# Adapter and expert products: the first product into one accumulator of 256 columns

## What is computed

```
y = einsum('bsi,boi->bso', x, weight[itok])      # x 8 x 256 x 1024, weight 8 x 1024 x 1024
base = einsum('bth,oh->bto', y, W_up)
top1 = argmax(y @ gate_w.T + expert_bias)
delta = ((y @ lora_A[e].T) @ lora_B[e].T for e = top1) # 4 experts, rank 8
out = x + base + delta
```

## Time and profile before

| | |
|---|---|
| three runs | 397.61, 398.24, 399.97 us |
| profiled execution, span from first to last instruction | 397.9 us |
| PE matmuls busy | 379.4 us (95%), 2240 instructions |
| PE weight loads busy | 355.0 us (89%), 2240 instructions |
| VectorE (DVE) busy | 213.9 us (54%) |
| ScalarE (ACT) busy | 145.4 us (37%) |
| GpSimd (POOL) busy | 17.5 us (4%) |

### The profile page before, as it was taken

How to read it: one execution, slowest core, us unless ns; L and a number is a source line. 1 busy time by engine, 2 the same in 40 slices (tenths; PEclk the granted TensorE clock), 3 DMA queues, 4 the chain that set the end, 5 groups by cost and what they waited for, 6 DMA issues and landing times.

```text
span 397.9 us, 6753 instructions
## 1 busy us (share of the span) xinstructions
PE 379.4 (95%) x2240; PEld 355.0 (89%) x2240; DVE 213.9 (54%) x484; ACT 145.4 (37%) x316; POOL 17.5 (4%) x17
## 2 busy tenths in 40 slices
PE   2899869999999999999999999999999999999996
PEld 2689759889998999889998899988999899988996
DVE  3768495645546347456366455473573553654132
ACT  4766620637015340356105470153503452053100
POOL 0007520000000000000000000000000000000000
PEclk9999988999999999999999999999999999999999
DMA  6897856652096322971257611864229712450002
GB/s 187 300 360 224 261 216 190 239 203 82 24 285 202 146 105 84 273 230 45 105 137 283 213 50 55 248 225 160 105 60 267 234 71 105 146 170 0 0 0 105
DMA packets 21365, 63.65 MB, mean 160 GB/s; under 512 B 2544, under 2 KB 3696, under 8 KB 21360
## 3 DMA queue, kind: packets, MB, share of 16 engines
q1 hardware_dynamic: 21072, 63.07, 47.8%
q10 hardware_dynamic: 288, 0.52, 0.4%
HBM read 55.20 MB, written 8.39 MB: 160 GB/s over the span
## 4 chain that ended last, share of the span: by engine, by line
PE 87%; DMA 4%; DVE 4%; ACT 2%; SPq 1%; issue 1%; POOL 1%; ACTq 0%
PE ps_o L461 31%; PE ps_y L450 28%; PE ps_y L452 14%; PE ps_o L470 13%; PE ps_o L485 2%; DMA w_raw<-w_dram 2%; DMA lb_raw<-lora_b_dram 2%; DVE w_lo L346 2%; DVE x_hilo L339 1%; ACT up_hi L280 1%; POOL up_lo L244 1%; PE ps_y L478 0%; SPq L133 0%; SPq L149 0%; SPq L197 0%
## 5 line engine op out<-in xcount | busy, mean ns | idle before, releaser
L450 PE MATMUL ps_y<-x_hilo,w_hi 128*128 128x512 f32 x512 | 180.3, 397 | 9.4 <-DVE w_lo L346 7.8
L452 PE MATMUL ps_y<-x_hilo,w_lo 128*128 128x256 f32 x512 | 142.7, 279 | 0.0
L450 PEld LDWEIGHTS ps_y<-x_hilo,w_hi 128*128 128x128 f32 x512 | 96.8, 189 | 32.7 <-issue 7.4
L452 PEld LDWEIGHTS ps_y<-x_hilo,w_lo 128*128 128x128 f32 x512 | 97.0, 189 | 0.0
L346 DVE TENSOR_TENSOR w_lo<-w_raw,w_hi 128x512 fp32r<-128x512 f32 x128 | 81.4, 686 | 3.5 <-ACT w_hi L276 1.3
L461 PE MATMUL ps_o<-up_hi,y_hi 128*128 128x366 f32 x256 | 75.9, 337 | 1.9 <-POOL up_lo L244 1.9
L461 PE MATMUL ps_o<-up_lo,y_hi 128*128 128x366 f32 x256 | 74.8, 333 | 0.0
L461 PE MATMUL ps_o<-up_hi,y_lo 128*128 128x366 f32 x256 | 74.8, 333 | 0.0
L276 ACT CAST w_hi<-w_raw 128x512 fp32r<-128x512 f32 x128 | 71.3, 621 | 2.3 <-DMA w_raw<-w_dram 2.1
L296 ACT COPY y_small<-ps_y 128x256 f32<-128x256 f32 x64 | 23.8, 372 | 121.4 <-PE ps_y L452 121.4
L396 DVE TENSOR_TENSOR y_full<-ps_y,y_small 128x256 f32<-128x256 f32 x64 | 27.1, 424 | 68.8 <-ACT y_small L296 68.8
(11 more groups left out here) (33 smaller groups left out, 177.8 us busy)
## 6 DMA issues: line engine op xcount, KB each, us to landing
w_raw<-w_dram SPq DMA_DIRECT2D x63, 512.0 KB, 4.1
rows<-x_dram SPq DMA_DIRECT2D x16, 512.0 KB, 5.3
x_raw<-xT_dram SPq DMA_DIRECT2D x30, 256.0 KB, 7.0
up_raw<-w_up_dram SPq DMA_DIRECT2D x8, 512.0 KB, 6.7
out_dram<-rows SPq DMA_DIRECT2D x8, 512.0 KB, 7.7
out_dram<-rows SPq DMA_DIRECT2D x8, 329.0 KB, 7.2
out_dram<-rows SPq DMA_DIRECT2D x8, 183.0 KB, 6.7
x_raw<-xT_dram ACTq DMA_DIRECT2D x2, 256.0 KB, 3.4
```

The lines of the kernel that those rows point to most:

```text
L450: pe.matmul(ps_y[c % 2][:, :], w_hi[:, c % RING, cols], x_hilo[:, k, :], start=(k == 0), stop=False)
L452: last = pe.matmul(ps_y[c % 2][:, S:2 * S], w_lo[:, c % RING, cols], x_hilo[:, k, 0:S], start=False, stop=(k == KC - 1))
```

## The change

The first product adds its three terms into one accumulator, 256 columns of the bank. A step is three matmuls of 256 columns, with w_hi, w_hi and w_lo as weights. `y_small` and `y_full` go, with their semaphores. ScalarE casts `y_hi` out of PSUM; VectorE takes `y_lo` as PSUM minus `y_hi`, and PE may write the bank again after `y_ready`.

```diff
 # ScalarE, per chunk
                     act.wait_ge(y_done, b * OC + c + 1)
-                    act.copy(y_small[:, c % 2, :], ps_y[c % 2][:, S:2 * S]).then_inc(y_small_ready, 1)
+                    act.copy(y_hi[:, c, :], ps_y[c % 2][:, 0:S]).then_inc(y_hi_ready, 1)
                     if c < OC - RING:
                         w_hi_part(b, RING + c)
-                    act.wait_ge(y_full_ready, b * OC + c + 1)
-                    act.copy(y_hi[:, c, :], y_full[:, c % 2, :]).then_inc(y_hi_ready, 1)
 # VectorE, per chunk
-                    dve.wait_ge(y_small_ready, b * OC + c + 1)
-                    if c >= 2 or not first:
-                        dve.wait_ge(y_hi_ready, b * OC + c - 1)
-                    dve.tensor_tensor(y_full[:, c % 2, :], ps_y[c % 2][:, 0:S], y_small[:, c % 2, :],
-                                      ALU.add).then_inc(y_full_ready, 1)
+                    dve.wait_ge(y_hi_ready, b * OC + c + 1)
+                    dve.tensor_tensor(y_lo[:, c, :], ps_y[c % 2][:, 0:S], y_hi[:, c, :].bitcast(F32),
+                                      ALU.subtract).then_inc(y_ready, 1)
                     if c < OC - RING:
                         w_lo_part(b, RING + c)
-                    dve.wait_ge(y_hi_ready, b * OC + c + 1)
-                    dve.tensor_tensor(y_lo[:, c, :], y_full[:, c % 2, :], y_hi[:, c, :].bitcast(F32),
-                                      ALU.subtract).then_inc(y_ready, 1)
 # TensorE, first_product
                     if c >= 2:
-                        pe.wait_ge(y_full_ready, b * OC + c - 1)
+                        pe.wait_ge(y_ready, b * OC + c - 1)
...
-                        pe.matmul(ps_y[c % 2][:, :], w_hi[:, c % RING, cols], x_hilo[:, k, :],
+                        pe.matmul(ps_y[c % 2][:, 0:S], w_hi[:, c % RING, cols], x_hilo[:, k, 0:S],
                                   start=(k == 0), stop=False)
-                        last = pe.matmul(ps_y[c % 2][:, S:2 * S], w_lo[:, c % RING, cols], x_hilo[:, k, 0:S],
+                        pe.matmul(ps_y[c % 2][:, 0:S], w_hi[:, c % RING, cols], x_hilo[:, k, S:2 * S],
+                                  start=False, stop=False)
+                        last = pe.matmul(ps_y[c % 2][:, 0:S], w_lo[:, c % RING, cols], x_hilo[:, k, 0:S],
                                          start=False, stop=(k == KC - 1))
```

More of the change, by code:

```diff
@@ L66, in build @@
         gl_raw = sb("gl_raw", [P, OC, GL])
-        y_small = sb("y_small", [P, 2, S])
-        y_full = sb("y_full", [P, 2, S])
         y_hi = sb("y_hi", [P, OC, S], F32R)
@@ L112, in build @@
         y_done = sem("y_done")
-        y_small_ready = sem("y_small_ready")
-        y_full_ready = sem("y_full_ready")
         y_hi_ready = sem("y_hi_ready")
```

## The result

The changed kernel takes 402.64 us (median of four runs, 401.99 to 404.35) against 398.73 us for the kernel before, whose median has a fourth run since: a ratio of 1.0105, with a 95% interval of 1.0076 to 1.0135. It is slower, by about 4 us, where 1.5 us less was forecast. That lies inside the range that the forecast gave, but on the side of its rival 1.

A forecast was written before the change was run, and what follows sets the result against it. PE bounds the kernel: batches 1 to 7 are matmuls end to end, 46.71 us a batch. 397.9 (span) - 1.2 (batch 0) - 0.2 (PE's stream) + 0.3 (span to median) = 396.8, said as 396.7; range 393.2 to 403.5.

The forecast's parts named there:

- rival 1: First product: weight load, not column count, sets the pace; 0.122 us a matmul, +8.6 us, 405.4; chance 0.22 in some strength.
- PE's stream: First product, batches 1 to 7: time goes by columns, three 256s at 0.1155 us, 0.3465 a step, -0.2 us in all.
- The bounds: First product, a 256 behind a 256: between 0.113 and 0.122 us, taken as 0.1155.
- Starts 0.12 us and more apart: Sign in the profile after: such starts in a row of 256s would prove the weight load sets the pace.
- rival 2: First product: pace falls to the load's own 0.113 us, -8 ns a step, -3.6 us, 393.4; chance 0.10.
- Batch 0: Without the join, ScalarE's up_hi casts and the up_lo chain come earlier: -1.2 us, bounds 0.8 to 1.9.
- The first half of the route: Batch 0: y_hi without the join lets up_hi casts start earlier; GpSimd's up_lo(3) ends at 34.9 instead of 36.08, 1.2 us.
- The second half of the route: Batch 0 behind up_lo(3): DMAs and all after move by 1.2 us; up_lo wait some 0.7, z_parts wait still 3.7.
- The covered join: Batches 1 to 7: the join's copy and add lie under a full PE, so removing them gains nothing.
- the bank's new wait: PE's wait for y_ready(c-2) in place of y_full_ready(c-2) comes no later than before.
- instruction supply: PE: 384 instead of 256 instructions per first product's 22 us, 58 ns each, costed at nothing.
- The fall of the clock: Batch 0, PE's z_parts wait: 3.7 us again with the same fall of the clock to 0.50.

The follow-up runs named there:

- width: Changed kernel with matmuls of 128 to 384 columns by chunk instead of 256, y incomplete or with foreign columns; one run, 415.03 us.
- bf16_join: Kernel before, with its join and matmuls of 512 and 256 columns, but w and x as bf16; 388.0 us, ratio 0.9749.
- hybrid: Batch 0 as in the changed kernel, batches 1 to 7 as in the kernel before; 397.27 us over 12 runs, ratio 0.9966.
- join_choose: Kernel before, join kept; in batch 0 x of batch 1 cast before the last W_up part, experts chosen before w_lo of batch 1; 392.85 us, ratio 0.9853.
- hybrid_choose: The hybrid; in batch 0 x of batch 1 cast before the last W_up part, experts chosen before w_lo of batch 1; 391.33 us, ratio 0.9823.
- before: The kernel before the change, with join and matmuls of 512 and 256 columns, as first profiled; median 398.73 us with a fourth run.
- after: First profile of the changed kernel, three matmuls of 256 columns a step and no join; median 402.64 us, ratio 1.0105.
- again: The changed kernel, unaltered, run and profiled a second time; 403.72 us, ratio 1.013 to the kernel before.
- split: Kernel before, join kept, with the matmul of 512 columns cut into two of 256 in 7 of 8 steps; 404.20 us, ratio 1.0147.
- bf16: Changed kernel with w and x, high and low parts, as bf16 instead of fp32r; one run, 387.89 us.
- bf16_width: Changed kernel with bf16 w and x and matmuls of 128 to 384 columns by chunk, y incomplete; one run, 382.06 us.
- reorder: Kernel before; in batch 0 up_hi cast ahead of y_hi, x of batch 1 ahead of the last up_hi, experts chosen before w_lo; 400.11 us, ratio 1.0042.

## Why the prediction was wrong, point by point

**PE's stream: the step that failed.** "... the split of the two starts leaves a fixed part of about nothing." I read the costs of the two kinds of matmul off the distances between their starts, 0.23 and 0.115 us, and took their ratio of 2 for proof that time goes by columns. But how a pair's time is split between two starts says little; only the sum over the pair is sound, 346.7 ns, and it holds 320 ns of columns and 26.7 ns for two matmuls. That could as well be 2 x 13.3, and it is (width; bf16_join shows the same with 2.5). The 512 more matmuls, 448 of them in batches 1 to 7, cost 448 x 13.0 = 5.8 us there, where I counted -0.2. The second product had a check in the chain of the earlier trace rows, which I did not make:

```profile
90.72 0.44 PE ps_o L470 x3
91.16 1.01 PE ps_o L461 x6
92.17 0.45 PE ps_o L470 x3
```

By columns at the first product's rate the three matmuls of 328 columns on the mean would take 0.444 us and the six of 366 0.991. They took 0.449 and 1.01, by which time does not go by columns alone. A fixed part of 13.3 ns gives 0.450 and 0.995, so the 366s hold still more than it.

**The bounds.** I bounded a 256 behind a 256 by 0.113 and 0.122 and took the middle; 0.120 lies inside, near the end that I gave 22%. The rival had the right sign, a size half as large again (its 8.6 us against 5.8) and the wrong cause: the load takes 110 ns, as the earlier trace rows said, and is hidden at 256. "Starts 0.12 us and more apart" came true and proved nothing of it, since a fixed part gives the same sign. I also had the loads start with the matmul before them, "the same to 0.01 us in rows 5"; the second pair there is 0.05 us apart. The rule of the Trainium skill that I weighed ("TensorE: Matmul & The Clock Gate", "Back-to-back issue gap") had the right form, a fixed part for each matmul, and I set it aside because its 2.5 ns was not what the rows held; they held 13.3 in another guise. The load of 107 ns that the same page of the Trainium skill gives (section "LDWEIGHTS") is 3 to 4% under the 110 to 111 measured in fp32r. Two slips in my sums change nothing in the forecast: by that rule the sum is 398.1 with the 0.3 us that I added to mine, and rival 2 is 393.4 in one place and 393.2 in another. The 0.003 us that I added in rival 1's 0.122 came from no row; without it that sum gives 0.119.

**Batch 0.** Forecast -1.2 us; hybrid 1.4 less (0.4 to 2.4), join_choose against hybrid_choose 1.2 to 1.5. The size agrees. The first half of the route is shown, if it is measured from the end of chunk 4, since that end itself moves from run to run. From ScalarE's first operation behind chunk 4 to the end of GpSimd's `up_lo(3)` it was 9.77 us with the join (before, 26.30 to 36.07; join_choose the same) and 8.54 or 8.55 without (after, again, hybrid, hybrid_choose): 1.23 us less, where I had 1.2. In the hybrid:

```profile
26.00 0.37 ACT L297 CAST y_hi<-ps_y 128x256 fp32r<-128x256 f32 x1 [1.47 <-PE ps_y L467]
28.68 5.87 POOL L244 TENSOR_TENSOR up_lo<-up_raw,up_hi 128x1024 fp32r<-128x1024 f32 x2 [1.09 <-ACT up_hi L280]
30.23 2.03 DVE L355 TENSOR_TENSOR up_lo<-up_raw,up_hi 128x1024 fp32r<-128x1024 f32 x1 [0.52 <-ACT up_hi L280]
```

VectorE's `up_lo(2)` is the one that is held up now, 2.03 us against 1.22 before, as I had written. In the first profile after, the gain does not show, because chunk 4 ended 1.2 us later than before (27.51 against 26.30; I put that down to the dearer matmuls and to the clock at 14 us, which is argued), so that `up_lo(3)` ended at 36.05, as before:

```profile
27.51 0.37 ACT L292 CAST y_hi<-ps_y 128x256 fp32r<-128x256 f32 x1 [1.47 <-PE ps_y L443]
30.19 5.86 POOL L240 TENSOR_TENSOR up_lo<-up_raw,up_hi 128x1024 fp32r<-128x1024 f32 x2 [1.07 <-ACT up_hi L276]
```

The second half of the route, that everything behind the DMAs moves by the same amount, is not shown: PE's wait for `up_lo` was 0, 0.7 and 0 us (after, again, hybrid) where I had 0.7, but the waits for `z_parts` were 3.2, 4.8 and 2.5 where I had 3.7, and the DMAs between vary by more than 1.2 us. For that half the agreement of the total may be luck.

The 5.8 us of batches 1 to 7 less the 1.4 of batch 0 are 4.4 us, and the two measured ratios of the changed kernel are 4.2 and 5.2 us.

**The covered join, the bank's new wait, instruction supply.** Right: neither profile of the changed kernel lists a wait of PE for `y_ready`, PE is busy from end to end in batches 1 to 7, and the two operations left take 24 and 27 us in all.

**The fall of the clock.** I counted it as the same in both kernels. It is not even the same in two executions of one kernel (after, again), which is why a single profile of batch 0 could have misled in either direction. And the 0.3 us between the span and the median had no meaning: in all runs on record the time lies 1.7 to 2.4 us above the span (402.23 for the span of 400.4), so the profiled execution, with its span of 397.9 us, took some 400 us, as the highest of the three runs did. The difference forecast does not hang on it.

## What to carry to other kernels

Where PE is busy from end to end, count its instructions as well as its columns: in this kernel's first product an fp32r matmul of 256 columns or more costs N / 2.4 + 13 ns, so one 512 is 13 ns cheaper than two 256s, and work saved on covered engines buys nothing back. Take a fixed cost from sums over a whole step, at two different numbers of instructions or two widths, never from how two starts divide the time between them. And look at the one batch where PE waits: two queues in another order there gave 1.5%, where taking the join out gave 0.3%. But trace first what stands behind each instruction that is moved: a `y_hi` two casts later cost PE a wait of 3.5 us for a bank.

## What the runs showed of the hardware

A matmul with fp32r operands, each with its own weight load, took 12.5 to 13.5 ns more than its columns at 2.4 GHz from 256 to 384 columns in the first product, one with bf16 operands 2.5 ns more from 128 to 384. The 13 ns are no constant of fp32r: in the second product of the same traces (fp32r, before) a 366 behind a 366 took 169.1 ns on the mean, 16.6 more than its columns, and the 128 of a transposition 61 ns, 7.5 more. In fp32r no row of matmuls with a load each went below 109 ns a matmul, the distance of its weight loads; in bf16 none was met at 56. Whether the 13 ns hang on the weights or on the moving operand, and whether they would go if two matmuls shared one load, stays open: neither was tried.

The granted clock fell to 0.50 during or just after a wait for `z_parts` of 3.7 us (before, split), 4.8 us (again), 3.5 us (bf16), 2.8 us (bf16_width) and 2.5 us (hybrid), and stayed at 1.00 through one of 3.2 us (after), 2.3 us (bf16_join) and 1.3 us (width). In reorder it stayed at 1.00 through a wait of 3.5 us and fell behind one of 1.8 us. So the length of the wait alone does not decide it. Without the wait for `z_parts` it was 0.999 to 1.000 on the mean in all five runs of hybrid_choose; in join_choose it was 0.996 in two of six, in the profiled one by a fall at 14.0 us, long before that place.

An operation of VectorE with both inputs in SBUF took far longer beside GpSimd's `up_lo`, one with an input in PSUM did not: `y_lo` took 1.67 us with two SBUF inputs and 2.42 in reorder, and in the changed kernel, as PSUM minus SBUF beside the same `up_lo`, 0.42:

```profile
30.80 0.42 DVE L388 TENSOR_TENSOR y_lo<-ps_y,y_hi 128x256 fp32r<-128x256 f32 x1 [0.38 <-ACT y_hi L292]
```
